# Mixture-of-experts stage on one core: block-wise waits in the second matmul, a third gather buffer, written-out expert loops

## The reference

```python
h = layernorm(x) * (1 + ca) + sa                 # x: 8 x 512 x 256, all of ca.. from silu(c) @ wmod
x = x + ga * linear_attention(h)                 # 16 heads of 16, chunks of 128
h = layernorm(x) * (1 + cb) + sb
weights = softmax over the top 2 of 8 experts of h @ emb.T
# each expert keeps its first 512 tokens (4096 tokens, 8 experts)
tokens = h_flat[index]                           # 8 x 512 x 256
inter = relu(tokens @ first_linear[e].T)         # 512 x 512
out = (inter @ second_linear[e].T) * vals        # 512 x 256
final = zeros.at[index].add(out)
x = x + gb * final
```

## Time and profile before

| | |
|---|---|
| runs | 458.04, 459.07, 461.75 us; median 459.07 |
| profiled execution | 458.25 us, its span 456.5 us |
| PE busy in the span | 396.4 us (87%) |
| PEld | 310.3 us (68%) |
| DVE | 335.2 us (73%) |
| ACT | 204.9 us (45%) |
| POOL | 236.0 us (52%) |
| DMA | 49.70 MB, mean 109 GB/s |

### The profile page before, as it was taken

One profiled execution on the slowest core, in us unless ns is written; L12 is line 12 of the kernel. 1 busy time (PEld: TensorE's weight loads), 2 busy tenths in 40 slices (PEclk: granted clock), 3 DMA queues, 4 the chain that ended last, 5 costly groups with the idle time before them and its releaser, 6 DMA issues. The chain is left out here.

```text
span 456.5 us, 9693 instructions
## 1 busy us (share of the span) xinstructions
PE 396.4 (87%) x3390; PEld 310.3 (68%) x3390; DVE 335.2 (73%) x877; ACT 204.9 (45%) x343; POOL 236.0 (52%) x299
## 2 busy tenths in 40 slices
PE   3696979999999998998998999997139999999981
PEld 0553757777776775786786788776129888888871
DVE  7573694998996996898998986988835665666540
ACT  1665335635543662572572580334106544444520
POOL 4124070483391491473474471375165888887444
PEclk9599899989979998999999995998559999999997
DMA  8201401503603602411521320437247898887333
GB/s 256 68 0 33 130 1 44 153 2 103 186 2 101 180 9 83 146 59 49 160 77 35 117 91 32 145 101 256 63 132 240 186 207 207 198 203 172 40 41 46
DMA packets 40868, 49.70 MB, mean 109 GB/s; under 512 B 6409, under 2 KB 33034, under 8 KB 40834
## 3 DMA queue, kind: packets, MB, share of 16 engines
q1 hardware_dynamic: 33666, 36.55, 25.1%
q0 software_dynamic: 7168, 12.72, 14.3%
HBM read 31.84 MB, written 17.42 MB: 108 GB/s over the span
## 5 line engine op out<-in xcount | busy, mean ns | idle before, releaser
L1627 DVE TENSOR_TENSOR sT<-quad,causal 128x1024 f32<-128x1024 f32 x64 | 74.6, 1206 | 1.3 <-PE quad L1125 1.3
L714 POOL DMA_INDIRECT out<-x,tok_i x32 | 52.5, 1641 | 21.3 <-DVE x L1947 14.6
L1125 PE MATMUL quad<-q_bd,kT 32*128 32x256 f32 x512 | 46.3, 409 | 7.4 <-DVE sT L1627 6.1
L611 POOL TENSOR_TENSOR x<-x_sb,bo_g 128x256 f32<-128x256 f32 x32 | 22.3, 730 | 45.9 <-issue 26.4
L703 POOL DMA_INDIRECT xg<-token_rows,tok_i x32 | 33.0, 1030 | 23.3 <-DVE tok_i L1916 11.9
L1157 PE MATMUL bank<-sT,v_pad 128*32 128x128 f32 x1024 | 44.1, 295 | 0.0
L1388 PE MATMUL bank<-w_hi,in_hi 128*128 128x256 f32 x128 | 37.0, 289 | 6.3 <-DVE in_lo L1932 6.3
L1125 PEld LDWEIGHTS quad<-q_bd,kT 32*128 32x128 f32 x512 | 27.2, 184 | 19.4 <-DVE sT L1627 11.9
L964 ACT ACTIVATE in_hi<-quad 128x512 fp32r<-128x512 f32 x32 | 19.1, 598 | 47.2 <-PE quad L1390 46.9
L1390 PE MATMUL bank<-w_lo,in_hi 128*128 128x256 f32 x128 | 36.2, 283 | 0.0
L1389 PE MATMUL bank<-w_hi,in_lo 128*128 128x256 f32 x128 | 36.2, 283 | 0.0
(11 more groups left out here) (225 smaller groups left out, 1032.1 us busy)
## 6 DMA issues: line engine op xcount, KB each, us to landing
x_sb<-x SPq DMA_DIRECT2D x8, 512.0 KB, 3.8
out<-x SPq DMA_DIRECT2D x8, 512.0 KB, 4.1
token_rows<-mod_all SPq DMA_DIRECT2D x8, 512.0 KB, 4.4
w_sb<-w1T SPq DMA_DIRECT2D x8, 512.0 KB, 4.5
w_sb<-w2T SPq DMA_DIRECT2D x8, 512.0 KB, 4.7
token_rows<-h SPq DMA_DIRECT2D x7, 528.0 KB, 3.1
rden<-rden_rows SPq DMA_DIRECT2D x56, 64.0 KB, 2.6
mod_all<-mod_rows SPq DMA_DIRECT2D x8, 384.0 KB, 5.0
```

What stands on the lines that cost most here:

```text
L611: ins = gp.tensor_tensor(x1[b.p][:, t, :], x_sb[b.p][:, t, :], bo_g[:, :], ALU.add)
L714: gp.indirect_dma_start(out=out_rows, out_offset=bass.IndirectOffsetOnAxis(ap=tok_i[:, 1, at:at + 1], axis=0), in_=y_sb[q][:, t, :], in_of ...
L1125: last = mm(quad[:, r, k * 2 * P:(k + 1) * 2 * P].rearrange("p (s i) -> p s i", s=2), kT[b.p][at, k, tok(t)], q_bd[b.p][at, k, :, tok(t)], ...
L1627: v.tensor_tensor(sT[t % 2][:, 8 * a:8 * (a + 1), :].rearrange("p (r s) i -> p r (s i)", s=2), quad[:, 2 * a:2 * a + 2, :].rearrange("p r ...
```

## The change

Three edits. `down` waits for `in_lo` block by block in its first tile instead of for all four blocks ahead of it. The gathered rows get three buffers instead of two, so `gather(e)` waits for expert e − 3, three gathers are issued first, and the scatters stand one expert later on GpSimd's queue. TensorE's and ScalarE's expert loops are written out in Python instead of running as hardware loops (VectorE's and SyncE's stay loops).

```diff
+ROW_BUFS = 3
-        xg = pair("xg", [P, SLOT_TILES, ROW])
+        xg = [sb(f"xg{r}", [P, SLOT_TILES, ROW]) for r in range(ROW_BUFS)]
...
             def gather(e):
-                q = e % 2
-                wait(gp, S["gT_mm"], KH * (e - 1))
-                wait(gp, S["aside_on"], e - 1)
+                r = e % ROW_BUFS
+                wait(gp, S["gT_mm"], KH * (e - ROW_BUFS + 1))
+                wait(gp, S["aside_on"], e - ROW_BUFS + 1)
...
-            gather(0)
-            gather(1)
-            for e in range(2, EXPERTS):
+            for e in range(ROW_BUFS):
                 gather(e)
-                scatter(e - 2)
-            scatter(EXPERTS - 2)
-            scatter(EXPERTS - 1)
+            for e in range(ROW_BUFS, EXPERTS):
+                gather(e)
+                scatter(e - ROW_BUFS)
+            for e in range(EXPERTS - ROW_BUFS, EXPERTS):
+                scatter(e)
...
-            next_expert(0, 0)
-            next_expert(1, 1)
-            with act.Fori(1, EXPERTS // 2 - 1) as i:
-                next_expert(2 * i, 0)
-                next_expert(2 * i + 1, 1)
-            next_expert(EXPERTS - 2, 0)
+            for e in range(EXPERTS - 1):
+                next_expert(e, e % 2)
...
             def down(e, q):
-                pe.wait_ge(S["in_lo_on"], IB * (e + 1))
                 pe.wait_ge(S["w_lo_on"], 2 * e + 2)
                 for t in range(SLOT_TILES):
 
                     wait(pe, S["y_on"], SLOT_TILES * e + t - 1)
                     for i in range(IB):
+                        if t == 0:
+                            pe.wait_ge(S["in_lo_on"], IB * e + i + 1)
...
-            with pe.Fori(1, EXPERTS // 2) as i:
-                up(2 * i - 1, 1)
-                turn_rows(2 * i, 0)
-                down(2 * i - 1, 1)
-                up(2 * i, 0)
-                turn_rows(2 * i + 1, 1)
-                down(2 * i, 0)
+            for e in range(1, EXPERTS - 1):
+                up(e, e % 2)
+                turn_rows(e + 1, (e + 1) % 2)
+                down(e, e % 2)
```

More of the change, by code:

```diff
@@ L336, in adaln_kernel @@
         w2_in = [sem(f"w2_in{q}") for q in range(2)]
-        gathered = [[sem(f"gathered{q}_{t}") for t in range(SLOT_TILES)] for q in range(2)]
+        gathered = [[sem(f"gathered{r}_{t}") for t in range(SLOT_TILES)] for r in range(ROW_BUFS)]
         SMALL = 18
@@ L703, in gather @@
                     gp.indirect_dma_start(
-                        out=xg[q][:, t, :], out_offset=None, in_=rows,
+                        out=xg[r][:, t, :], out_offset=None, in_=rows,
                         in_offset=bass.IndirectOffsetOnAxis(ap=tok_i[:, 0, at:at + 1], axis=0),
-                        bounds_check=TOKENS - 1, oob_is_err=False).then_inc(gathered[q][t], 16)
+                        bounds_check=TOKENS - 1, oob_is_err=False).then_inc(gathered[r][t], 16)
             def scatter(e):
@@ L939, in turn_rows @@
                 wait(act, S["y_on"], SLOT_TILES * (e - 1))
-                act.activation(aside[q][:, :, :], xg[q][:, :, ROW_W:ROW], ACT.Copy).then_inc(S["aside_on"], 1)
+                act.activation(aside[q][:, :, :], xg[e % ROW_BUFS][:, :, ROW_W:ROW], ACT.Copy)\
+                    .then_inc(S["aside_on"], 1)
             def first_rows():
@@ L1393, in turn_rows @@
                 wait(pe, S["x_lo_on"], KH * e)
+                r = e % ROW_BUFS
                 for t in range(SLOT_TILES):
-                    wait(pe, gathered[q][t], loads_of(e, q))
+                    pe.wait_ge(gathered[r][t], 16 * (e // ROW_BUFS + 1))
                     for k in range(KH):
-                        last = nc.tensor.transpose(bank[k][:, tok(t)], xg[q][:, t, k * P:(k + 1) * P],
+                        last = nc.tensor.transpose(bank[k][:, tok(t)], xg[r][:, t, k * P:(k + 1) * P],
                                                    ident[:, :])
```

## The result

| | before | after |
|---|---|---|
| median of 18 runs each | 459.0 us (450.2 to 461.8) | 460.6 us (456.7 to 465.0) |
| ratio of the undisturbed runs | 1 | 1.0134, 95% interval 1.0101 to 1.0167 |
| profiled execution, its span | 458.25 us, 456.5 | 458.17 us, 456.4 |
| first gather starts | 332.78 us | 330.10 us |
| from the first gather to the end of the span | 123.7 us | 126.3 us |

A forecast was written before the change was run, and what follows sets the result against it. TensorE was taken to set the pace, waiting on in_lo, with GpSimd full as well. TensorE −7.6, GpSimd's tail +4.9, net −2.7 from 458.25 gave 455.5; the median forecast was 455.7 us, range 451.3 to 459.3.

The forecast's parts named there:

- Block by block: TensorE's second matmuls of experts 0 to 6 start 1 us earlier; TensorE and the last y 7.6 us sooner.
- Loops at no cost: TensorE's and ScalarE's written-out loops: priced at 0, 3.5 us if some three further blocks each stalled for a code packet.
- The tail: GpSimd's scatters 4 to 7 stand together, each block waiting for the one before to land: 10.2 us per step.
- The holds: VectorE's w_lo holds GpSimd's descriptors, 0.39 us each: 3.9 us before scatter 4, 1.0 in the tail.
- the rival in which GpSimd stays free: Gathers not held by w_lo, or no holds at all: 450.6 to 453.3 us; chance 0.30.
- Where GpSimd's schedule starts: GpSimd's gather and scatter blocks up to scatter 4 priced by its own time: 56.8 us from 348.7, so 405.5.
- The sum's other term: TensorE and the last y come 7.6 us sooner.
- the small gain: Whole kernel: net −2.7 us, from TensorE's −7.6 and 4.9 given back at GpSimd's tail.
- The last line of the sum: Whole kernel: 455.5 us for the profiled execution, median of the runs 0.8 above that execution, forecast 455.7.
- The rival for slower: Each w_lo holds GpSimd 1.05 us, +8.8 us in all, end +6.0: 464.3; chance 0.06, 0.05 by over 1%.

The follow-up runs named there:

- wait_only: The kernel before with only the block-by-block wait on in_lo; loops, two buffers and GpSimd's order unchanged: ratio 0.9951 to the kernel before.
- old_order_new_tail: As order_of_before, but gather 7 stands ahead of scatter 4, so scatters 4 to 7 follow each other: ratio 1.0118 to the kernel before.
- pause_in_series: The change, but the third block of gathers waits for expert 0's aside: eight gathers, a pause, eight more; ratio 1.0041 to the kernel before.
- thin_first_up: The change, but expert 0's first matrix leaves out the two low-part products, 16 matmuls instead of 48; run once for its trace, last in_lo at +14.9.
- order_of_before: The change with its three buffers, but gathers and scatters in the order of the kernel before: ratio 1.0019 to the kernel before.

## Why the prediction was wrong

Its steps, one by one.

*Block by block: right.* The wait ahead of the second matmul in the change, by line and shape, beside the earlier trace rows:

```profile
L1386 PE MATMUL bank<-w_hi,in_hi 128*128 128x256 f32 x128 | 38.3, 300 | 5.8 <-DVE in_lo L1929 4.1 <-issue 1.7
...
L1386 PEld LDWEIGHTS bank<-w_hi,in_hi 128*128 128x128 f32 x128 | 24.8, 194 | 7.2 <-issue 5.5 <-DVE in_lo L1929 1.3 <-DVE x L1944 0.2
...
L1396 PE MATMUL bank<-ident,xg 128*128 128x128 f32 x56 | 7.2, 272 | 0.0
```

Of the 5.8 us, 5.4 are the three gaps of expert 0, where the relu itself came late; experts 1 to 6 have none, and expert 7 has 0.35 (0.7 was said). The period is 12.3 us (12.1 was said). In wait_only TensorE's last matmul comes 5.8 us sooner than before; 7.6 was taken, from the weight loads, and 6.0 is what the matmul row gave. The matmul row was the better reading.

*Loops at no cost: right* (0.9994, at most 1.0038).

*The tail: right.* Scatters 4 to 7 start 10.22, 10.68 and 10.23 us apart (10.2, and 1.0 of holds in all, was said). The waits of some 3 us and their cause are in old_order_new_tail.

*The holds: right in size.* From scatter 0 to scatter 4 the change takes 55.2 us (412.62 − 357.42); 51.4 without holds and 3.9 of holds, 55.3, was said. Gathers are held too, so the rival in which GpSimd stays free has fallen.

*Where GpSimd's schedule starts: wrong, and with it the sum.* The prediction let scatter 0 follow the sixteenth gather at once: the third and the fourth block were priced by GpSimd's own time alone, and it said of the third buffer that it "frees no wait of TensorE". It asked which waits the earlier gathers would free, and not what sixteen in a row would do to others. Scatter 0 started 6.1 us after that point. Scatter 7 was forecast at 441.1, +108.3 from the first gather; it came at +113.7. The 5.3 us between the two are these 6.1, less 0.8 in the other steps. The sum's other term fails by the same step: TensorE and the last y were to come 7.6 us sooner, and TensorE's last matmul came 1.9 us later than before, since the relus of expert 0 had to wait for the signals; by its y alone scatter 7 could not have started before +113.0. Whether the small gain would have stood without the late signals, no run shows. The kernels with two buffers and the block wait have one (0.5 and 1.0%); pause_in_series, with three buffers and no stall at the first relus, has none (scatter 7 at +112.9), and some of its signals are late further on.

*The last line of the sum* does not follow from it: 455.5 for the profiled execution and 0.8 for the median make 456.3, not 455.7. Either lies 4 to 5 us under the measured median.

*The rival for slower* had the sign and not the mechanism: it needed larger holds, and these were as forecast.

What stays open is the path on which a series of gathers delays TensorE's signals. Weights, bytes and a full DMA are excluded. The length of the series matters; that TensorE's own rate of matmuls matters too rests on thin_first_up alone, which also moved the blocks. Every execution here was recorded, so whether an unrecorded one would show it, no run can say. The Trainium skill ("Perfetto Trace Analysis", Tensor Engine Instruction (MATMUL, LD_WEIGHTS)) says that a matmul's row ends, by an estimate, before its signal is pushed and made visible, and that agrees with rows which end 4.7 to 7.6 us before anyone acts on them; it gives no length for that time. The Trainium skill also says ("NOTIFIC — the notification-queue block", 7.1, Overflow) that the block which writes the records holds back its producers rather than lose a record inside it; no run here shows whether that happens.

## What to carry to other kernels

A deeper buffer is also a new order on the queue that fills it: price what now runs without a pause, and whose signals that delays, and not only which waits go. Try a relaxed wait with the old order first (here: two buffers, 0.5 to 1.0% faster; three, 0.6 to 1.3% slower). Where a full engine is held by another one's long instruction, cut that instruction: four pieces cost VectorE 0.2 us more, and a hold fell from up to 1.0 us to 0.25.

## What was not expected of the hardware

TensorE's signals can lag its matmuls while GpSimd issues an unbroken series of indirect gathers of 1.00 us at 0.30 us spacing: in the blocks of the first matrix by 4.7 to 7.6 us with sixteen (the change) and by 2.5 to 4.5 with twelve (order_of_before). The last of them is acted on some 2 us after the last gather's descriptor ends (+20.9 and +22.9 in the change, +15.7 and +17.5 in order_of_before). The signals of ScalarE and VectorE in the same stretch came at once (in_lo at 349.96, TensorE at 350.10). A pause of 2.3 us after eight gathers kept the signals of the first matrix in time; two of the second matrix, in the eight gathers behind the pause, were some 4 and 7 us late. So the number of gathers in a row is not the whole condition. A subtraction with two inputs in SBUF holds a gather as it holds a scatter, at 0.12 to 0.13 us into the descriptor, and between two such subtractions GpSimd gets in.
